# Half of the wide x refills issued by ScalarE on a queue of its own

## The reference

```python
h = x                                    # x: (512, 39, 16)
for i, S in enumerate([128, 128, 128]):
    Wr = Ws[i].reshape(39, h.shape[1], S)
    out = relu(einsum('bfd,bgd,fgs->bsd', x, h, Wr) + bs[i][None, :, None])
    if i != 2:
        h, direct = out[:, :S // 2], out[:, S // 2:]
    else:
        direct = out
    outs.append(direct)
return sum(concatenate(outs, axis=1), axis=-1)   # (512, 256)
```

## Time and profile before

| | |
|---|---|
| Time, median of 3 runs | 617.93 us (617.48 to 617.95) |
| The profiled execution's own time | 617.64 us |
| Span of its profile | 615.8 us |
| PE busy | 565.6 us, 92% |
| DVE busy | 533.5 us, 87% |
| POOL busy | 517.9 us, 84% |
| ACT busy | 376.3 us, 61% |
| DMA queue q1 (all of SP's loads) | 87.7% of 16 engines' span, 118.57 MB |

### The profile page before, as it was taken

How to read it: one execution, slowest core, us unless ns; L and a number is a source line. 1 busy time by engine, 2 the same in 40 slices (tenths; PEclk the granted TensorE clock), 3 DMA queues, 4 the chain that set the end, 5 groups by cost and what they waited for, 6 DMA issues and landing times.

```text
span 615.8 us, 8529 instructions
## 1 busy us (share of the span) xinstructions
PE 565.6 (92%) x2032; PEld 386.3 (63%) x2032; DVE 533.5 (87%) x514; ACT 376.3 (61%) x421; POOL 517.9 (84%) x231
## 2 busy tenths in 40 slices
PE   0658368999999999999999999999999999999997
PEld 0325235666676667667676767767666766777665
DVE  2426609999999989899999999999999999999975
ACT  1423514857667576758576676757676675767653
POOL 0345556898998989898998989898989989898995
PEclk9797697999999999999999999999999999999999
DMA  8999985999999999999999999999999999986001
GB/s 207 238 217 237 224 189 141 193 238 191 231 205 206 211 210 218 175 223 189 224 212 202 217 203 230 197 226 197 220 197 222 201 197 218 204 213 151 0 2 34
DMA packets 33071, 118.74 MB, mean 193 GB/s; under 512 B 6817, under 2 KB 6945, under 8 KB 30928
## 3 DMA queue, kind: packets, MB, share of 16 engines
q1 hardware_dynamic: 33056, 118.57, 87.7%
HBM read 118.02 MB, written 0.52 MB: 192 GB/s over the span
## 4 chain that ended last, share of the span: by engine, by line
PE 80%; DMA 8%; SPq 5%; issue 3%; POOL 1%; DVE 1%; ACT 1%; POOLq 0%; DVEq 0%; ACTq 0%
PE acc L458 80%; SPq L247 4%; DMA xwide<-x 4%; DMA xshift<-x 2%; DMA xrep<-x 2%; POOL z_lo L220 1%; DVE z_raw L343 1%; SPq L236 0%; SPq L230 0%; DVE z_whole L343 0%; SPq L280 0%; ACT h L528 0%; ACT last L528 0%; DVE z_psum L343 0%; ACT z_hi L525 0%
## 5 line engine op out<-in xcount | busy, mean ns | idle before, releaser
L220 POOL TENSOR_TENSOR z_lo<-z_raw,z_hi 128x1024 fp32r<-128x1024 f32 (+2 forms) x224 | 512.0, 2325 | 82.1 <-ACT z_hi L525 81.9
L525 ACT CAST z_hi<-z_raw 128x1024 fp32r<-128x1024 f32 (+2 forms) x224 | 225.8, 1018 | 154.2 <-DVE z_raw L343 137.4
L343 DVE TENSOR_TENSOR z_raw<-h,xwide 128x1024 f32<-128x1024 f32 x192 | 230.9, 1218 | 27.1 <-DMA xwide<-x 13.4
L458 PE MATMUL acc<-z_hi,w_hi 128*128 128x512 f32 (+2 forms) x560 | 224.2, 470 | 12.9 <-ACT z_hi L525 6.6
L458 PE MATMUL acc<-z_hi,w_lo 128*128 128x512 f32 (+2 forms) x560 | 184.1, 398 | 0.0
L458 PE MATMUL acc<-z_lo,w_hi 128*128 128x512 f32 (+1 forms) x528 | 172.7, 401 | 9.8 <-POOL z_lo L220 5.2
L458 PEld LDWEIGHTS acc<-z_hi,w_hi 128*128 128x128 f32 (+2 forms) x560 | 106.6, 191 | 76.1 <-issue 47.9
L458 PEld LDWEIGHTS acc<-z_hi,w_lo 128*128 128x128 f32 (+2 forms) x560 | 106.4, 190 | 28.8 <-issue 3.8
L458 PEld LDWEIGHTS acc<-z_lo,w_hi 128*128 128x128 f32 (+1 forms) x528 | 99.0, 189 | 38.9 <-POOL z_lo L220 10.6
L458 PE MATMUL acc<-z_whole,w_whole 128*128 128x512 f32 x256 | 121.5, 597 | 0.0
L458 PE MATMUL acc<-z_whole,w 117*128 117x512 f32 x128 | 65.6, 637 | 24.2 <-DVE z_whole L343 24.2
(11 more groups left out here) (16 smaller groups left out, 90.3 us busy)
## 6 DMA issues: line engine op xcount, KB each, us to landing
xwide<-x SPq DMA_DIRECT2D x320, 256.0 KB, 13.5
xshift<-x SPq DMA_DIRECT2D x45, 546.0 KB
xrep<-x SPq DMA_DIRECT2D x48, 78.0 KB
xwide<-w SPq DMA_DIRECT2D x2, 1024.0 KB, 23.2
xshift<-x SPq DMA_DIRECT2D x3, 312.0 KB
xshift<-x SPq DMA_DIRECT2D x3, 234.0 KB
w_whole<-w_rest SPq DMA_DIRECT2D x1, 512.0 KB, 18.3
w<-w0a SPq DMA_DIRECT2D x1, 409.5 KB
```

Of the source, the lines that this page charges most:

```text
L220: return eng.tensor_tensor(lo[0:rows, 0:n, :], z[0:rows, 0:n, :], hi[0:rows, 0:n, :].bitcast(F32), ALU.subtract)
L343: nc.vector.tensor_tensor(dst, in0, in1, ALU.mult).then_inc(made[kind], 1)
L458: return nc.tensor.matmul(dst, w[0:rows, PLACE[layer, t], :], z[0:rows, t - G * g, :], start=first and t == 0, stop=final and t == TILES[l ...
L525: nc.scalar.copy(z_hi[0:rows, slot("PV", pair, par, pos, HI_RING), 0:n, :], src).then_inc(hi_made, 1)
```

## The change

`load_wide` becomes a function of both engines. In the steps' refills SP issues only e = 0 (the lower 64 partitions). ACT issues e = 1 (the upper 64) on its own queue: in its walk over the positions, after the cast of a layer-2 group (or, for a group of kind "W", which has no cast, in that group's place), it waits for the same product semaphore that SP waits for, and issues the DMA. The first loads of both halves, `xrep`, `xshift` and the weights stay on SP. Both DMAs still add 16 to the same semaphore, and DVE still waits for 32 per refill.

```diff
+        def load_wide(eng, j, half, g, e):
+            first = T12 * e + G * g
+            if (g, e) != (G12 - 1, 1):
+                run = [[1, G * N]]
+            else:
+
+                run = [[(FIELDS + T12 - 1 - first) * N, G], [1, N]]
+            src = bass.AP(x2.tensor, x2.offset + ROWS2 * N * j + N * first, [[0, HALF]] + run)
+            eng.dma_start(xwide[HALF * e:HALF * (e + 1), half, G * g:G * (g + 1), :],
+                          src).then_inc(xw_in[half][g], 16)
...
                     if layer == 2 and not (isinstance(j, int) and j + 1 >= BLOCKS):
 
                         sp.wait_ge(made[kind], before(kind, j, pos) + 1)
-                        load_wide(j + 1, par, g)
+                        load_wide(sp, j + 1, par, g, 0)
...
             for g in range(G12):
-                load_wide(0, 0, g)
+                for e in range(2):
+                    load_wide(sp, 0, 0, g, e)
...
                     if kind != "W":
                         high_part(pair, par, pos)
+                    if layer == 2 and has(0, BLOCKS - 2):
+
+                        act.wait_ge(made[kind], before(kind, j, pos) + 1)
+                        load_wide(nc.scalar, j + 1, par, g, 1)
```

More of the change, by code:

```diff
@@ L236, in load_shift @@
                     sp.dma_start(xshift[a * FIELDS:(a + 1) * FIELDS, ts[0]:ts[-1] + 1, :], src).then_inc(landed, 16)
[L238 to L248, removed]
             def refill(pair, par):
@@ L284, in _ @@
                     sp.wait_ge(w_lo_made, len(SPLIT0) + 1)
-                load_wide(1, 1, g)
+                for e in range(2):
+                    load_wide(sp, 1, 1, g, e)
             refill(-1, 1)
```

## The result

The changed kernel takes 636.35 us (median of 5 runs, 633.42 to 637.28) against 617.48 us of the kernel before beside it (614.88 to 617.95): a ratio of 1.0296, 95% interval 1.0268 to 1.0323. It is slower by 3%, and outside my range of 617.0 to 630 us. The profiled execution took 633.42 us, 15.8 more than that of before.

What follows compares the result with a forecast made beforehand. PE was taken to bound the kernel. Issues 0, waits 0, xshift of step 1 +0.6 and unrolled steps +0.1 gave 617.64 + 0.7 = 618.3, 618.6 on the median's scale; forecast 618.4 us, range 617.0 to 630.

Steps and rivals of the forecast that it cites:

- TensorE bounds the middle: From 131.97 us on: 458.08 us of matmuls in one piece, 34.2 us a step, all PE; faster loads cannot shorten it.
- ScalarE's issues are hidden: ACT's chain from relu0 to the next step's first cast: DMA issues fit while the engine works, cost 0.
- The issuers collide: Rival at ACT's relu1: SP and ACT issues collide, relu1 0.1 to 0.4 us late beyond the reserve; about 621 us, chance 0.14.
- xshift of step 1, +0.6: First layer-0 product of step 1: ACT's refill of g0 shares DMA engines with xshift, delaying it 0.6 us, once.
- my bound: Delay of step 1's xshift: 1.4 us at 186 GB/s, or 0 if g0's part moves in what xshift leaves free.
- The 0.1 for unrolled steps: Steps 1 and 2, where PE had no reserve: +0.1 us in the sum.
- What DVE does wait for is `xwide`, 7.3 us in 9 waits, which does not reach PE.: Steps after step 1: DVE's waits for refills, 7.3 us in all, were taken not to delay PE.
- what was to spare (0.28 us): ACT and POOL chain up to position 6: room before PE reads the result, 0.28 us a step; anything beyond lengthens every step.
- the order rival: g5 at position 6: ACT's upper parts pass xshift and g5's lower part, which lands later; 627 us, chance 0.13.
- The net 1 us a step: Order of transfers at g5: 2 to 3 us for upper parts ahead, less the relief, nets 1 us a step, 14 in all.
- The credit of 4.7 us: Lead of g5's cast over TensorE, 336.48 - 331.82 = 4.7 us, subtracted from the 14 us of later g5 landings.
- the form that I chose: The main forecast for the whole kernel: issues hidden on ACT, 617.2 to 619.8 us, chance 0.55.

Runs made afterwards that it cites:

- e4: Kernel before (SP issues all refills), plus a 4 KB DMA issued by ScalarE at each of the changed kernel's places, with a wait before it; 622.04 us, 1.0054.
- e2: Changed kernel with ScalarE issuing the upper halves of g5 to g9 only, SP all other refills; 633.6 us, 1.026.
- e6: Changed kernel with xrep and xshift issued behind SP's refill of g5 instead of ahead of it, from step 1 on; 658.51 us, 1.0647.
- e7: Kernel before, SP issuing every refill, with xrep and xshift issued behind the refill of g5 from step 1 on; 621.83 us, 1.0053.
- e3: Changed kernel with the lower half of g5 also issued by ScalarE, so all of g5 is on ScalarE's queue; 620.85 us, 1.0036.
- e9: Changed kernel with ScalarE also issuing xrep and xshift from step 1 on, so the upper half of g5 stands behind xshift; 624.4 us, 1.0081.

## Why the prediction was wrong

1. *TensorE bounds the middle* was right for the kernel before. I concluded that only its own chain counts, and that is where it begins to fail.
2. *ScalarE's issues are hidden* held. They are where I placed them, inside the casts and relu0, and the chain of the earlier trace rows is 6.12 us against 6.13. e4 puts their cost at some 0.5%, 0.8% at most.
3. *The issuers collide* (621): not on ScalarE. One of its issues takes 482 ns in the median (472 to 663) beside SP's 469, and relu1 isn't late. On SP the six issues ahead of g5 take 0.3 us longer. That isn't what costs the 3%: in e2 they take 2.54 us, less than before, and its step is 35.42 all the same.
4. *xshift of step 1, +0.6*: -0.2 us measured from issue to product, so nothing. The value of 0 in my bound was the right one. The 0.1 for unrolled steps can't be told from 0.
5. **The step that failed** is "What DVE does wait for is `xwide`, 7.3 us in 9 waits, which does not reach PE." The waits didn't reach TensorE, but what they meant did: DVE waited in most steps because landing and work, 33.99 us, made a loop of nearly its whole period of 34.20. In ten of the twelve steps the product starts 0.11 us after the landing, as in all twelve steps of the changed kernel: the loop was closed before the change already. It fitted under TensorE's step, 34.3 us and not the 34.2 that I had worked out, by 0.2 us. I had counted the wait and not the loop. With TensorE's chain I asked what was to spare (0.28 us); with DVE's I didn't.
6. *The price of the order rival*, 14 - 4.7 = 9 us, was mis-sized in one term, though its place, its sign and its mechanism are what happened. The net 1 us a step was right: it measured 12 x 1.13 = 13.6 us over steps 2 to 13. The credit of 4.7 us wasn't there. It was also read at the wrong link, since TensorE waits for POOL's remainder: the cast ends at 331.82, POOL needs 2.41 us and TensorE reads the result at 337.41, which leaves 3.2 us at best. And the earlier trace rows show the lead of a step in the middle, when DVE has been ahead for long. In step 1 of the kernel before, the cast of position 8 ends 0.70 us before TensorE needs it, and this grows to 4.4 us by step 3; in the changed one it is 0.05 us in step 1 and 1.1 in step 3. A reserve that is built up by the difference of two rates doesn't exist once the rates turn round.
7. Without the credit the rival's sum would have been 618 + 14 = 632, and the profiled execution took 633.42. The other runs are up to 4 us longer; of those there is no trace here. A chance of 0.13 was too low: the rows for it (g5 behind `xshift`, a wait of 0.72 us that comes back every step) were stronger than those of the form that I chose.

The page "DMA: Bandwidth & Descriptors" of the Trainium skill, section "Queues, rings and completion order", has the queues served in turn, packet by packet. The traces agree: in the stretch above SP's queue sent 334 packets and ScalarE's 273, though the bytes were 2.16 and 0.88 MB, and e6 against e7 shows the price.

Beside the earlier trace rows the prediction took the rule on ports from the page "SBUF — State Buffer" of the Trainium skill, section "Door 1: The DMA port swizzle (why `[64,N]` ≈ `[32,N]`)", and I inferred from it that two queues, one for the lower and one for the upper side, would move the refills faster. From the issue of g5 to its product the rate is 187 GB/s before and 189 after, the means of twelve steps, so in the changed kernel the measurement decides against it. In e3 (203) and e9 (198) it was 6 to 9% higher than before; whether the ports have to do with that isn't shown.

## What to carry to other kernels

One DMA queue is also an order of priority. Whoever moves a part of its transfers to another engine's queue gives up that order: what was behind now shares with what is urgent, whatever the engines' own time. Before such a change, find the transfer with no time to spare (a wait that comes back every step, however short), add its landing to the work between its use and its next issue, and compare the sum with the step; if they are equal, each microsecond of delay is one a step, and a lead seen in the middle is no reserve against it. Count the bytes ahead of that transfer over several steps, and look at the packets: beside a transfer with long rows, a queue of short ones gets the smaller share of the bytes.

## What I had not expected of the hardware

- Two queues moved no more than one where it counted: 189 GB/s against 187 from the issue of g5 to its product, and 182 in e6 against 188 in e7 from the issue of `xshift` to its use (means of twelve steps). Two other orders did move more, 203 in e3 and 198 in e9. Single stretches scatter from 173 to 202 GB/s within the kernel before, so a pair of them proves nothing.
- ScalarE's sequencer issues a DMA while its engine is in the middle of a cast (326.33 within the cast of 326.18), and the engine's next instruction starts as soon as without it.
- A transfer at the head of a second queue (e3) took 16.3 us to land. In e6, ahead of `xshift` in the first queue, it took 4.8. Behind the difference are the packets: while `xshift` with its 14 KB rows is under way, ScalarE's queue sends nearly as many packets as SP's (96 to 132) and less than a third of its bytes.
